# Selective scan: the column-order C values cross memory by 4-byte writes and whole-row reads instead of whole-row writes and 32-byte reads

## The chip, the cores and the metric

The kernel runs on one core of a Trainium2 chip. The metric is the device time of one launch in microseconds (us), lower is better. A launch computes the whole batch of 8 images, one image after the other.

## The reference

The input is `x` of 8 x 192 x 64 x 64 floats. Layer 0 is a state-space block: a layer norm over the channels, a projection to 384 channels (192 for the scan, 192 for a gate), a 3x3 depthwise convolution, and then a selective scan over the 4096 pixels in four directions. Layer 1 is a non-local attention block over the same pixels. What matters here is the scan:

```python
x_hw = xc.reshape(Bsz, D, L)                          # pixels row by row
x_wh = xc.transpose(0, 1, 3, 2).reshape(Bsz, D, L)    # pixels column by column
xs = jnp.stack([x_hw, x_wh, x_hw[..., ::-1], x_wh[..., ::-1]], axis=1)
x_dbl = jnp.einsum('kcd,bkdl->bkcl', x_proj_w, xs)
dts, Bv, Cv = jnp.split(x_dbl, [R, R + N], axis=2)    # 12, 4 and 4 rows per direction
...
dA = jnp.exp(dt_t[..., None] * A)
h = dA * h + dt_t[..., None] * B_t[:, :, None, :] * u_t[..., None]
y = jnp.einsum('bkdn,bkn->bkd', h, C_t)
```

For each direction k and each pixel there are four values C (one per state), the same for all 192 channels. Directions 0 and 2 go over the rows of the picture, directions 1 and 3 over its columns.

## The kernel before, in words

An image goes through three stages with a barrier behind each: project and scan, mix (output projection, and the projections of the attention), attend. The scan works in 32 chunks of 512 pixels: `ORDER = (0, 2, 1, 3)` gives the directions, 8 chunks each. A chunk's place in this list is called `at`. Places 0 to 15 (`at < EV`) are the row directions, where a chunk is 8 rows of the picture; places 16 to 31 are the column directions, where it is 8 columns.

`run_chunks` writes the code of each engine's `body` out 32 times; every engine has its own fixed order, and semaphores tie them. In `body(at)`:

- PE (TensorE) makes the projected rows of place at+2 (`xdbl`, only while at+2 < 16), the time-step rows (`dtproj`), spreads the C rows of this place over all 128 partitions (`spread`, line 478: a selection matrix times the tile `xhl[at % 2]`) and sums the products over the states.
- ACT (ScalarE) copies the small rows of place at+2 out of PSUM (`copy_xd`, line 786), computes the decay factors (`decay`, line 824), and copies the rows into `xhl` (`copy_high`, line 797). `xhl` holds in one tile the high part of the C rows and, 64 partitions further, the rest that DVE subtracts in `low_half` (line 1154). So there are two sets of rows, high and low.
- POOL (GpSimd) finishes the time step of place at+1 (`residue`, line 1011), multiplies it by the input (`times_u`, line 1017), and multiplies that by the spread B rows, in three `drive` operations (line 1026).
- DVE (VectorE) runs six scans (line 1175) and three products with C (line 1183) a chunk, and between them one step of the softplus for the next place (`softplus`, line 1165).
- SP issues every DMA. For each place it writes the four B rows to memory (line 329, tensor `rows`, with a wait for that write in line 330), and reads them back spread over 128 partitions (lines 332 and 335, tile `bs`).

The projection of a row chunk also yields the C values of directions 1 and 3 for the same pixels, 2 x 4 rows in both the high and the low set. They are kept in memory until the column directions need them. `STORE = (3, 5, 7, 9, 11, 13, 14, 15)` are the eight places at which SP stores a chunk of them to the tensor `ct` of 16 rows x 4096 pixels: two DMAs of 8 rows (line 339), issued once `low_half` of this place is done. At places 16 to 31 SP reads 4 + 4 of these rows for 8 columns of the picture back into `xhl` (line 350), once PE has finished reading the tile for place at-2 (the count of `cbc_ready`).

Three waits hang on the stores. SP itself goes on with the B rows of the next place only after it has issued the store. ACT may not overwrite `xhl` in `copy_high(at + 2)` until the store of place at has landed (`c_stored1`). At place 16 SP waits for all stores of the image before the first read. ACT's `copy_xd(at)` in turn waits until the B rows of place at-1 have been written out (`rows_saved`), and POOL's first `drive` of a place waits until its `bs` tile has been loaded (`b_loaded`).

Of the kernel before, what the change touches and what calls it, by code (L numbers as in the profile page):

```python
# [19 lines left out]
F32 = mybir.dt.float32  # L20
# [5 lines left out]
B, C, HH, WW = 8, 192, 64, 64  # L26
L = HH * WW
P = 128
R = C - P
NS, RANK, K = 4, 12, 4  # L30
O = 96
T = 512
NCH = L // T
RPC = T // WW
# [5 lines left out]
EV = 2 * NCH  # L40
STORE = (3, 5, 7, 9, 11, 13, 14, 15)
# [13 lines left out]
def build(nc, nb, x, vec, w_in, w_x, w_dt, sel, fold, ident, w_out, w_att, gb, w_w, out):  # L55
# [3 lines left out]
    with ctx:  # L59
# [29 lines left out]
        selr = sb("selr", [P, NT * P], F32R)  # L89
# [21 lines left out]
        def flat(ap):  # L111
            return ap.rearrange("p (a b) -> p a b", b=WW)
# [49 lines left out]
        xhl = [sb(f"xhl{i}", [P, T], F32R, where=scx) for i in range(2)]  # L162
# [6 lines left out]
        h = sb("h", [P, NT, T], where=scx)  # L169
# [3 lines left out]
        ps = ctx.enter_context(nc.psum_tensor("ps", [P, 8, T], F32))  # L173

        rden = nc.dram_tensor("rden", [T], F32, kind="Internal").ap()
        ct = nc.dram_tensor("ct", [4 * NS, L], F32, kind="Internal").ap()
# [39 lines left out]
        for w, rows_ in ((wx0, slice(0, P)), (wx1, slice(P, 2 * P))):  # L216
            for s, k in enumerate((0, 2)):
                at = s * P
# [73 lines left out]
        @block.sync  # L292
        def _(sp):
            sp.wait_ge(S["pads_set"], 11)
            for dst, src in LOADS:
                sp.dma_start(dst, src).then_inc(s_load, 16)
            sp.wait_ge(s_load, NL)
            barrier(sp, 0, -1)

            def load(im, i, c, q):  # L300

                sp.wait_ge(S["x_free"], i + 1)
                sl = bass.ds(c * T, T)
                sp.dma_start(xa[:, q, :], xr[im, 0:P, sl]).then_inc(S[f"x_loaded{q}"], 16)
                sp.dma_start(xb[0:R, q, :], xr[im, P:C, sl]).then_inc(S[f"x_loaded{q}"], 16)

            for q in range(2):
                load(0, q, q, q)
            with sp.Fori(0, nb) as b:
                sp.wait_ge(S["out_stored"], b * (32 * NCH) + 32)  # L310
                sp.sem_inc(mark, 1)
                with sp.Fori(1, NCH // 2) as cc:
                    for q in range(2):
                        load(b, (b * 2) * NCH + cc * 2 + q, cc * 2 + q, q)
                sp.wait_ge(S["xc_ready"], b * NCH + NCH)
                sp.sem_inc(mark, 1)

                def body(at, par, g, before, now, nxt, after):
                    k, c = now
                    if at < EV:  # L320
                        sp.wait_ge(S["xd_ready"], b * EV + (at + 1))
                        src = xd[RANK:RANK + NS, :]
                    else:
                        if at == EV:
                            sp.wait_ge(S["xs_ready"], b * NCH + NCH)
                        m = LO + 16 * (k // 2) + RANK
                        src = xsf[m:m + NS, bass.ds(c * T, T)]
                    sp.wait_ge(S["dbu_ready"], g * NP + 1)
                    sp.dma_start(rows[par], src).then_inc(S["rows_saved"], 16)
                    sp.wait_ge(S["rows_saved"], g * 16 + 32)  # L330
                    whole = rows[par].rearrange("n t -> (n t)").unsqueeze(0).to_broadcast([P, NS * T])
                    sp.dma_start(bs[par][:, 0:2, :, :].rearrange("p q e t -> p (q e t)"), whole).then_inc(S[f"b_loaded{par}"], 16)
                    for half in range(2):
                        part = rows[par].rearrange("(e w) t -> w e t", w=2)[half:half + 1].to_broadcast([R, 2, T])
                        sp.dma_start(bs[par][half * R:half * R + R, 2, :, :], part).then_inc(S[f"b_loaded{par}"], 16)
                    if at in STORE:
                        sp.wait_ge(S["xlo_ready"], b * EV + (at + 2))
                        for m, row in ((0, NX), (2 * NS, R + NX)):
                            sp.dma_start(ct[m:m + 2 * NS, c * T:(c + 1) * T], xhl[par][row:row + 2 * NS, :].bitcast(F32))\
                                .then_inc(S[f"c_stored{par}"], 16)  # L340
                    if at >= EV:
                        if at == EV:
                            sp.wait_ge(S["c_stored0"], b * 32 + 32)
                            sp.wait_ge(S["c_stored1"], b * (32 * 7) + 32 * 7)
                        sp.wait_ge(S["cbc_ready"], g * NP + 1)
                        for m, row in ((0, RANK + NS), (2 * NS, R + RANK + NS)):
                            m += NS * (k // 2)
                            src = ct[m:m + NS, :].rearrange("r (h w) -> r h w", w=WW)[:, :, c * RPC:(c + 1) * RPC]
                            dst = xhl[par][row:row + NS, :].bitcast(F32).rearrange("p (h w) -> p h w", w=RPC)
                            sp.dma_start(dst, src).then_inc(S[f"c_loaded{par}"], 16)  # L350
                run_chunks(sp, b, body)
                barrier(sp, b, 0)
                with sp.Fori(0, NCH // 2) as cc:
                    for q in range(2):
                        load(b, (b * 2 + 1) * NCH + cc * 2 + q, cc * 2 + q, q)
                barrier(sp, b, 1)
                for q in range(2):
                    load((b + 1) % nb, (b * 2 + 2) * NCH + q, q, q)

                def store(c):  # L360
                    sp.wait_ge(S["fin_ready"], (b * NCH + c) * 2 + 4)
                    sl = bass.ds(c * T, T)
                    sp.dma_start(outr[b, 0:P, sl], fa[:, 0, :]).then_inc(S["out_stored"], 16)
                    sp.dma_start(outr[b, P:C, sl], fa[0:R, 1, :]).then_inc(S["out_stored"], 16)

                def attend(c, par, before, nxt):

                    i = b * NCH + c
                    d = b * (NCH - 1) + c
                    if before:  # L370
                        sp.wait_ge(S["yraw_ready"], i + 1)
                        sp.dma_start(dcol[:, :], yraw[O:O + 1, :].rearrange("o (p j) -> o p j", j=4)).then_inc(S["den_loaded"], 16)
                        sp.wait_ge(S["rden_ready"], i)
                        sp.dma_start(rden.rearrange("(p j) -> p j", j=4), rcol[:, :]).then_inc(S["den_saved"], 16)
                        sp.wait_ge(S["den_saved"], d * 16)
                        sp.dma_start(rdb[:, :], rden.unsqueeze(0).to_broadcast([O, T])).then_inc(S["rb_loaded"], 16)
                        store(c - 1)
                    if nxt:
                        sp.wait_ge(S["nmx_ready"], i + 2)
                        for t in range(4):  # L380
                            sp.dma_start(thc[1 - par][0][O:O + 1, t * P:(t + 1) * P].bitcast(F32), nmr[:, t:t + 1].bitcast(F32))\
                                .then_inc(S["shift_loaded"], 16)
                run_attend(sp, attend)
                store(NCH - 1)
                barrier(sp, b, 2)
            sp.wait_ge(S["out_stored"], nb * (32 * NCH) + 32)
            for q in range(2):
                sp.wait_ge(S[f"x_loaded{q}"], nb * (32 * NCH) + 32)
# [3 lines left out]
        def _(pe):  # L392
            mm = pe.matmul
# [9 lines left out]
            with pe.Fori(0, nb) as b:  # L403
# [64 lines left out]
                def spread(q, k, c, at, g):  # L468

                    pe.wait_ge(S["hc_ready"], g * NP + (q + 3))  # L470
                    if q == 0 and at < EV:
                        pe.wait_ge(S["xlo_ready"], b * EV + (at + 2))
                    if q == 0 and at >= EV:
                        pe.wait_ge(S[f"c_loaded{at % 2}"], b * (32 * NCH) + 32 * ((at - EV) // 2 + 1))
                    for e in range(2):
                        j = 2 * q + e
                        src = flat(xhl[at % 2][:, :]) if at < EV else xhl[at % 2][:, :].rearrange("p (h w) -> p w h", w=RPC)
                        m = mm(flat(ps[:, 4 + e, :]), selr[:, j * P:(j + 1) * P], src, start=True, stop=True)  # L478
                    m.then_inc(S["cbc_ready"], 1)

                def sum_first(k, c, g):
# [236 lines left out]
        def _(act):  # L718
# [10 lines left out]
            with act.Fori(0, nb) as b:  # L729
# [62 lines left out]
                def copy_high(at, g):  # L792

                    act.wait_ge(S["cbc_ready"], g * NP + 1)
                    if at - 2 in STORE:
                        act.wait_ge(S["c_stored1"], b * (32 * 7) + 32 * (STORE.index(at - 2) + 1))
                    A(xhl[at % 2][:, :], ps[:, 0, :], ACT.Copy).then_inc(S["xhi_ready"], 1)

                def soft_abs(g):
# [642 lines left out]
```

## Time and profile before

| | us |
|---|---|
| median of 3 runs | 9575.38 (9568.02 to 9575.95) |
| the profiled execution, device time | 9585.77 |
| the profiled execution, span of the trace | 9583.9 |
| TensorE busy | 8813.6 (92%) |
| VectorE busy | 7318.6 (76%) |
| ScalarE busy | 6190.6 (65%) |
| GpSimd busy | 3294.3 (34%) |

The span runs from the first to the last instruction; the device time has 1.9 us more around it. The shares are averages over stages of different kinds: in the attention TensorE is busy all the time and GpSimd does nothing, in the scan VectorE and GpSimd carry much more than their average. The first image takes about one eighth of the span, its scan lies between 175 and 640 us from the start, and the other seven repeat it.

### The profile page before, as it was taken

The numbers are of one execution on the slowest core, as the hardware profiler recorded it, in microseconds if no ns is written. First come the engines' busy times: TensorE is split into PE (matmuls) and PEld (weight loads), VectorE is DVE, ScalarE is ACT, GpSimd is POOL, SyncE is SP. The second block draws the span as 40 slices with busy tenths as digits, with TensorE's granted clock in tenths as the row PEclk, the third lists the DMA queues.
The fourth block names the chain that finished last, engine by engine and source line by source line (L and its number), as shares of the span: only waits on it lengthen the run. The fifth ranks groups of instructions, "written<-read, shape, count | busy, mean of one in ns | idle before, by whom it ended". The sixth has DMA issues, their size and how long they took to land. (4 is left out here: it accounts for less than half of the span.)

```text
span 9583.9 us, 104556 instructions
## 1 busy us (share of the span) xinstructions
PE 8813.6 (92%) x26564; PEld 4729.1 (49%) x26564; DVE 7318.6 (76%) x8161; ACT 6190.6 (65%) x7500; POOL 3294.3 (34%) x1874
## 2 busy tenths in 40 slices
PE   7899988999889998899988999889998899989999
PEld 3336733367333673336733367333673336633366
DVE  6977769777697767977679776797767977679776
ACT  6765667656676566755667656675566755677555
POOL 2860028500385003850038500385003850048400
PEclk9999999999999999999999999999999999999999
DMA  1320013200132002320013200132002320023200
GB/s 52 114 77 12 11 54 112 72 12 11 54 114 72 11 10 61 109 71 11 12 59 113 68 10 12 59 114 67 10 12 63 110 67 10 12 66 114 60 11 12
DMA packets 286701, 503.35 MB, mean 53 GB/s; under 512 B 142155, under 2 KB 143215, under 8 KB 253431
## 3 DMA queue, kind: packets, MB, share of 16 engines
q1 hardware_dynamic: 286199, 497.81, 17.4%
q8 instruction: 174, 2.85, 0.1%
q14 instruction: 328, 2.69, 0.1%
HBM read 467.99 MB, written 29.47 MB: 52 GB/s over the span
## 5 line engine op out<-in xcount | busy, mean ns | idle before, releaser
L1313 DVE TENSOR_TENSOR pl<-pf,ph 128x1024 fp32r<-128x1024 f32 x1024 | 1254.6, 1225 | 1014.1 <-ACT ph L961 1006.3
L1175 DVE TENSOR_TENSOR_SCAN h<-ps,h,dbu 128x512 f32<-128x512 f32 x1536 | 1886.8, 1268 | 65.9 <-POOL dbu L1026 29.9
L1026 POOL TENSOR_TENSOR dbu<-bs,du 128x1024 f32<-128x1024 f32 x768 | 1800.9, 2375 | 54.1 <-POOL du L1017 54.1
L961 ACT ACTIVATE ph<-pf 128x1024 fp32r<-128x1024 f32 x1024 | 1086.5, 1061 | 753.0 <-PE ps L652 752.7
L955 ACT ACTIVATE pf<-ps 128x1024 f32<-128x1024 f32 x1024 | 1051.5, 1027 | 534.9 <-PE ps L639 534.9
L981 POOL MEMSET sqb<- 64x512 f32 x16 | 8.3, 520 | 3998.1 <-issue 3993.2
L824 ACT ACTIVATE ps<-dt,negA 128x512 f32<-128x512 f32 x1536 | 1038.3, 688 | 494.5 <-DVE h L1175 494.1
L1297 DVE TENSOR_REDUCE mx<-ps 128x1 f32<-128x512 f32 x1792 | 1168.9, 684 | 78.4 <-PE ps L557 60.4
L1183 DVE TENSOR_TENSOR hc<-h,ps 128x1024 f32<-128x1024 f32 x768 | 938.0, 1221 | 194.9 <-PE ps L478 113.5
L478 PE MATMUL ps<-xhl,selr 128*128 128x512 f32 x1536 | 847.8, 639 | 147.7 <-DVE hc L1183 147.5
L1011 POOL TENSOR_TENSOR dt<-dt,ze 128x1024 f32<-128x1024 f32 x256 | 605.9, 2367 | 923.7 <-ACT dt L817 923.5
L1017 POOL TENSOR_TENSOR du<-dt,u 128x512 f32<-128x512 f32 x512 | 714.3, 1417 | 567.2 <-DVE dt L1165 566.6
L637 PE MATMUL ps<-thc,phh 97*128 97x512 f32 x2048 | 845.7, 413 | 6.7 <-ACT thc L938 6.7
L650 PE MATMUL ps<-ph,gth 128*97 128x512 f32 x2048 | 817.4, 399 | 11.7 <-DVE pl L1313 8.6
L638 PE MATMUL ps<-thc,phl 97*128 97x512 f32 x2048 | 815.3, 398 | 0.0
L639 PE MATMUL ps<-thc,phh 97*128 97x512 f32 x2048 | 812.9, 397 | 0.0
L652 PE MATMUL ps<-pl,gth 128*97 128x512 f32 x2048 | 808.6, 395 | 0.0
L651 PE MATMUL ps<-ph,gtl 128*97 128x512 f32 x2048 | 807.5, 394 | 0.0
L557 PE MATMUL ps<-phh,thc 96*128 96x512 f32 x1824 | 633.6, 408 | 45.2 <-POOLq L187 18.8
L478 PEld LDWEIGHTS ps<-xhl,selr 128*128 128x128 f32 x1536 | 271.3, 196 | 631.0 <-DVE hc L1183 370.5
L505 PE MATMUL ps<-hc,foldw 128*128 128x512 f32 x1024 | 548.1, 662 | 0.0
L489 PE MATMUL ps<-hc,eye 128*128 128x512 f32 x1024 | 484.3, 595 | 0.0
(191 smaller groups left out, 14691.2 us busy)
## 6 DMA issues: line engine op xcount, KB each, us to landing
bs<-rows SPq DMA_DIRECT2D x256, 1024.0 KB, 5.2
bs<-rows SPq DMA_DIRECT2D x512, 256.0 KB, 6.1
xa<-in_x SPq DMA_DIRECT2D x130, 256.0 KB, 2.9
xb<-in_x SPq DMA_DIRECT2D x130, 128.0 KB, 3.0
out<-fa SPq DMA_DIRECT2D x64, 256.0 KB, 2.1
rdb<-rden SPq DMA_DIRECT2D x56, 192.0 KB, 3.4
out<-fa SPq DMA_DIRECT2D x64, 128.0 KB, 2.4
xhl<-ct SPq DMA_DIRECT2D x256, 8.0 KB
```

Of the source, the lines that this page charges most:

```text
L478: m = mm(flat(ps[:, 4 + e, :]), selr[:, j * P:(j + 1) * P], src, start=True, stop=True)
L637: mm(dst, kk, thc[par][0][:, :], start=True, stop=False)
L638: mm(dst, phl[:, m * P:(m + 1) * P], thc[par][0][:, :], start=False, stop=False)
L650: mm(dst, gth[:, m, :], ph[:, mp % 2, e, :], start=(m == 0), stop=False)
L824: A(ps[:, 2 + e, :], dt[par][:, 0 if j < NS else 1, :], ACT.Exp, scale=negA[:, k * NT + j:k * NT + j + 1]).then_inc(S["dA_ready"], 1)
L955: A(pf[:, mp % 2, :, :], ps[:, 2 * (mp % 2):2 * (mp % 2) + 2, :], ACT.Exp)\
L961: A(ph[:, mp % 2, :, :], pf[:, mp % 2, :, :], ACT.Copy).then_inc(S["ph_ready"], 1)
L1026: pool.tensor_tensor(dbu[:, q, :, :], bs[par][:, q, :, :], du[:, r:r + 1, :].to_broadcast([P, 2, T]), ALU.mult).then_inc(S["dbu_ready"], 1)
L1175: dve.tensor_tensor_scan(h[:, j, ::step], ps[:, 2 + e, ::step], dbu[:, q, e, ::step], h[:, j, end:end + 1], ALU.mult, ALU.add)\
L1183: TT(hc[:, q, :, :], h[:, 2 * q:2 * q + 2, :], ps[:, 4:6, :], ALU.mult).then_inc(S["hc_ready"], 1)
L1297: dve.tensor_reduce(mx[:, t, m:m + 1], ps[:, 5 + j % 2, :], AX.X, ALU.max)\
L1313: TT(pl[:, mp % 2, :, :], pf[:, mp % 2, :, :], ph[:, mp % 2, :, :].bitcast(F32), ALU.subtract)\
```

## The change

A store no longer writes rows of 512 pixels in picture order. It writes each value to its place in column order, so that `ct` holds the 4096 pixels of each row column by column. Neighbours of a source row are 64 values apart in memory, so every piece written is one value of 4 bytes. Each of the 16 rows of a store has a DMA of its own (16 DMAs of 512 pieces in place of 2 DMAs of 8 rows). The read at places 16 to 31 becomes a plain read of 4 rows of 512 values. The chunk then lies in `xhl` in column order, and the `spread` matmul reads it straight, where it used to step through it with a stride of 8 values. The counts of the semaphores `c_stored0` and `c_stored1` follow the number of DMAs.

```diff
@@ SP, body
                     if at in STORE:
                         sp.wait_ge(S["xlo_ready"], b * EV + (at + 2))
                         for m, row in ((0, NX), (2 * NS, R + NX)):
-                            sp.dma_start(ct[m:m + 2 * NS, c * T:(c + 1) * T], xhl[par][row:row + 2 * NS, :].bitcast(F32))\
-                                .then_inc(S[f"c_stored{par}"], 16)
+                            for n in range(2 * NS):
+                                dst = ct[m + n:m + n + 1, :].rearrange("r (w h) -> r h w", h=HH)[0, c * RPC:(c + 1) * RPC, :]
+                                src = xhl[par][row + n:row + n + 1, :].bitcast(F32).rearrange("p (h w) -> p h w", w=WW)
+                                sp.dma_start(dst.unsqueeze(0), src, allow_slow_non_contiguous=True).then_inc(S[f"c_stored{par}"], 16)
                     if at >= EV:
                         if at == EV:
-                            sp.wait_ge(S["c_stored0"], b * 32 + 32)
-                            sp.wait_ge(S["c_stored1"], b * (32 * 7) + 32 * 7)
+                            sp.wait_ge(S["c_stored0"], b * 256 + 256)
+                            sp.wait_ge(S["c_stored1"], b * (256 * 7) + 256 * 7)
                         sp.wait_ge(S["cbc_ready"], g * NP + 1)
                         for m, row in ((0, RANK + NS), (2 * NS, R + RANK + NS)):
                             m += NS * (k // 2)
-                            src = ct[m:m + NS, :].rearrange("r (h w) -> r h w", w=WW)[:, :, c * RPC:(c + 1) * RPC]
-                            dst = xhl[par][row:row + NS, :].bitcast(F32).rearrange("p (h w) -> p h w", w=RPC)
-                            sp.dma_start(dst, src).then_inc(S[f"c_loaded{par}"], 16)
+                            src = ct[m:m + NS, c * T:(c + 1) * T]
+                            sp.dma_start(xhl[par][row:row + NS, :].bitcast(F32), src).then_inc(S[f"c_loaded{par}"], 16)
@@ PE, spread
                     for e in range(2):
                         j = 2 * q + e
-                        src = flat(xhl[at % 2][:, :]) if at < EV else xhl[at % 2][:, :].rearrange("p (h w) -> p w h", w=RPC)
-                        m = mm(flat(ps[:, 4 + e, :]), selr[:, j * P:(j + 1) * P], src, start=True, stop=True)
+                        m = mm(ps[:, 4 + e, :], selr[:, j * P:(j + 1) * P], xhl[at % 2][:, :], start=True, stop=True)
@@ ACT, copy_high
                     if at - 2 in STORE:
-                        act.wait_ge(S["c_stored1"], b * (32 * 7) + 32 * (STORE.index(at - 2) + 1))
+                        act.wait_ge(S["c_stored1"], b * (256 * 7) + 256 * (STORE.index(at - 2) + 1))
```

On SP's queue, at place 13 and up to the B rows of place 15, this stood before (`ct<-xhl` is the store, `rows<-xd` and `bs<-rows` the B rows of the place that follows; in brackets the semaphore that a DMA waits for):

```order
L339 DMA ct<-xhl1 8x512 [waits xlo_ready]
L339 DMA ct<-xhl1 8x512
L328 ISA [waits xd_ready]
L329 DMA rows0<-xd 4x512 [waits dbu_ready]
L330 ISA
L332 DMA bs0<-rows0 128x2048 [waits rows_saved]
L335 DMA bs0<-rows0 64x2x512 x2
L337 REGISTER_ALU
L339 DMA ct<-xhl0 8x512 [waits xlo_ready]
L339 DMA ct<-xhl0 8x512
L328 ISA [waits xd_ready]
L329 DMA rows1<-xd 4x512 [waits dbu_ready]
```

And this stands there now:

```order
L342 DMA ct<-xhl1 8x64x1 [waits xlo_ready]
L342 DMA ct<-xhl1 8x64x1 x15
L328 ISA [waits xd_ready]
L329 DMA rows0<-xd 4x512 [waits dbu_ready]
L330 ISA
L332 DMA bs0<-rows0 128x2048 [waits rows_saved]
L335 DMA bs0<-rows0 64x2x512 x2
L337 REGISTER_ALU
L342 DMA ct<-xhl0 8x64x1 [waits xlo_ready]
L342 DMA ct<-xhl0 8x64x1 x15
L328 ISA [waits xd_ready]
L329 DMA rows1<-xd 4x512 [waits dbu_ready]
```

The B rows of places 14 and 15 stand behind 16 DMAs each where they stood behind 2; nothing changed its place. At place 16, the first of a column direction, SP's queue before had the reads of C in 64 pieces of 8 values a row:

```order
L335 DMA bs0<-rows0 64x2x512 x2
L343 REGISTER_ALU
L344 ISA [waits c_stored0]
L350 DMA xhl0<-ct 4x64x8 [waits cbc_ready,c_stored1]
L350 DMA xhl0<-ct 4x64x8
```

and now it has whole rows:

```order
L335 DMA bs0<-rows0 64x2x512 x2
L345 REGISTER_ALU
L346 ISA [waits c_stored0]
L351 DMA xhl0<-ct 4x512 [waits cbc_ready,c_stored1]
L351 DMA xhl0<-ct 4x512
```

The reads stand where they stood, with the same waits. The order on PE, ACT, POOL and DVE is the same as before.

## Rows read from the trace of the kernel before

**Rows 1.** The page: span, and busy time of each engine.

```profile
span 9583.9 us, 104556 instructions
PE 8813.6 (92%) x26564; PEld 4729.1 (49%) x26564; DVE 7318.6 (76%) x8161; ACT 6190.6 (65%) x7500; POOL 3294.3 (34%) x1874
```

**Rows 2.** Busy time of each engine in stretches (row and column places, first image).

```profile
core 0: us, PE busy (x) PEld busy (x) DVE busy (x) ACT busy (x) POOL busy (x), PEclk, DMA share, GB/s
219.00:391.00 172.00, 152.11 (x357) 63.10 (x356) 165.20 (x144) 133.67 (x185) 140.08 (x73) 1.00 0.34 112
420.00:636.00 216.00, 201.69 (x388) 74.57 (x386) 196.74 (x168) 159.08 (x194) 185.50 (x91) 0.97 0.34 104
```

**Rows 3.** SP in order of time, first image, places 7 and 13 to 15.

```profile
start us, us, engine line op out<-in xcount [idle before <-releaser]
275.38 0.61 SPq L339 DMA_DIRECT2D ct<-xhl  x2
279.41 0.24 SPq L329 DMA_DIRECT2D rows<-xd  x1
280.79 0.34 SPq L332 DMA_DIRECT2D bs<-rows  x1
281.18 1.24 SPq L335 DMA_DIRECT2D bs<-rows  x2
...
304.27 0.61 SPq L339 DMA_DIRECT2D ct<-xhl  x2
...
362.33 0.61 SPq L339 DMA_DIRECT2D ct<-xhl  x2
...
376.82 0.61 SPq L339 DMA_DIRECT2D ct<-xhl  x2
...
391.32 0.61 SPq L339 DMA_DIRECT2D ct<-xhl  x2
```

**Rows 4.** DMA issues of the page: size, median us from issue to landing.

```profile
bs<-rows SPq DMA_DIRECT2D x512, 256.0 KB, 6.1
```

**Rows 5.** POOL in order of time: places 8 and 14 to 16.

```profile
291.54 2.34 POOL L1011 TENSOR_TENSOR dt<-dt,ze 128x1024 f32<-128x1024 f32 x1
296.26 2.50 POOL L1017 TENSOR_TENSOR du<-dt,u 128x512 f32<-128x512 f32 x2 [2.39 <-DVE dt L1165]
299.01 7.03 POOL L1026 TENSOR_TENSOR dbu<-bs,du 128x1024 f32<-128x1024 f32 x3 [0.25 <-POOL du L1017]
...
400.49 7.03 POOL L1026 TENSOR_TENSOR dbu<-bs,du 128x1024 f32<-128x1024 f32 x3 [0.17 <-POOL du L1017]
...
416.47 7.02 POOL L1026 TENSOR_TENSOR dbu<-bs,du 128x1024 f32<-128x1024 f32 x3 [0.25 <-POOL du L1017]
```

**Rows 6.** DVE, then ACT, in order of time, beside these.

```profile
294.87 1.22 DVE L1165 SCALAR_TENSOR_TENSOR dt<-ps,dt 128x1024 f32<-128x1024 f32 x1
...
293.10 0.57 ACT L786 ACTIVATE xd<-ps 20x512 f32<-20x512 f32 x1
```

**Rows 7.** Issue time on SP in ns (least, median, most) of three lines.

```profile
L339 SPq DMA_DIRECT2D ct<-xhl x128: 268/290/298, 217.3 to 8738.8; - x128
...
L350 SPq DMA_DIRECT2D xhl<-ct x256: 622/640/731, 405.0 to 8968.8; - x128
...
L381 SPq DMA_DIRECT2D thc<-nmr x224: 516/596/1554, 821.3 to 9515.2; - x112
```

**Rows 8.** DMA between 420 and 423.5 us (two reads of C).

```profile
DMA packets 520, 0.02 MB, mean 5 GB/s; under 512 B 520, under 2 KB 520, under 8 KB 520
q1 hardware_dynamic: 520, 0.02, 8.3%
```

**Rows 9.** DMA between 217.5 and 219.5 us (two stores of C).

```profile
q1 hardware_dynamic: 32, 0.03, 9.1%
```

**Rows 10.** Who waited for whom: DVE, 420 to 636 us.

```profile
DVE hc L1183 <- PE ps L478: 13.2, 14, 1.5
```

**Rows 11.** The spread matmul in a row place and in a column place.

```profile
285.76 1.03 PE L478 MATMUL ps<-xhl,selr 128*128 128x512 f32 x2
...
417.96 1.03 PE L478 MATMUL ps<-xhl,selr 128*128 128x512 f32 x2
```

## The prediction

> **What bounds the kernel now.** I read the page first: TensorE is busy 92% of the span, the others less [rows 1]. That average belongs mostly to the attention, which the change does not touch, so the next view is the busy time by stretch. In the row places of the scan VectorE is busy 165.20 of 172.00 us and GpSimd 140.08 [rows 2]: DVE sets the pace, one place in about 14.5 us (the stores at 275.38 and 304.27 are two places apart [rows 3]). In the column places DVE is busy 196.74 of 216.00 us. Who waited for whom says why: 13.2 us of that is DVE waiting for the spread matmul, in 14 waits [rows 10].
>
> Then the queue that the change fills, SP in order of time. At place 7 the store takes 0.61 us, from 275.38; SP then waits, issues the B rows of place 8 at 279.41 and their spread reads until 282.42 (281.18 + 1.24) [rows 3]. The last read lands 6.1 us after its issue [rows 4], that is at 281.80 + 6.1 = 287.9, 8.5 us after the B rows were issued. The first user is POOL's `drive` of place 8, which begins at 299.01 [rows 5]. So the queue has some 11 us of slack, and what matters is how much of it the store eats.
>
> How much may POOL be late? It has an idle gap of 2.39 us a place, but in front of `times_u`, where it waits for DVE's line 1165. From `drive` it runs without a gap into the next `residue`; one such is 291.54 to 293.88, and DVE's line 1165, which needs it, starts at 294.87 [rows 5, 6]. So the slack is 1.0 us: a `drive` over 1.0 us late stops DVE, and DVE has nothing to give back.
>
> **The change, part by part.** Call S the time that SP needs to issue one store, now 0.61 us, then 16 DMAs of 512 pieces each.
>
> *An isolated store (places 3, 5, 7, 9, 11).* The B rows of the next place are issued at 275.4 + S, landed 8.5 us later, and needed at 299.0 + 1.0 = 300.0. Free up to S = 16.1; beyond that each us of S is a us of DVE. There are five, since the slip also moves the next store and the time until it, 28.9 us, lets the queue recover. ACT's `copy_xd` of place 9 starts at 293.10 and needs the B rows of place 8 saved, 1.4 us after their issue: that begins to slip at S = 16.3, the same point, and is no separate cost [rows 3, 6].
>
> *The three stores at the end (13, 14, 15).* They stand one place apart, 362.33, 376.82, 391.32 [rows 3]. Between two stores SP needs 3.0 us for the B rows (282.42 - 279.41), so from S = 11.5 the second and third start late. The B rows of place 15 land at 362.3 + S + 3.0 + S + 8.5 = 373.8 + 2S against 400.5 + 1.0; those of place 16 at 362.3 + 3S + 6.0 + 8.5 = 376.8 + 3S against 416.5 + 1.0 [rows 5]. The second rules: a loss of 3S - 40.7 from S = 13.6 on, which takes in what place 13 loses. It is paid once an image, since behind it SP has no stores and recovers.
>
> So an image loses 5 x (S - 16.1) + (3S - 40.7) us, and there are eight.
>
> *S itself.* No row shows DMAs of 512 single values. A DMA of 8 pieces takes 290 ns to issue, one of 256 pieces 640 ns [rows 7]: 1.41 ns a piece, and 1.00 us for 512, S = 16.0. Line 381 writes 128 single values in 596 ns [rows 7]: 2.55 ns a piece beyond the 8, and 1.58 us for 512, S = 25.2. If the pieces cost the queue nothing, S = 16 x 0.29 = 4.6, the lower end. I take 1.2 us a DMA, between the two and nearer to the row with 256 pieces, the nearest to 512 in count: S = 19.2.
>
> *The transfers.* Two reads of C make 520 packets: 512 pieces and 4 completions a DMA of 4 rows [rows 8]. Two stores make 32: 16 rows and 8 completions a DMA of 8 rows [rows 9]. So a DMA runs on as many of the 16 DMA engines as its outer dimension has entries, and the new one (8 x 64 x 1) on 8: 64 pieces each, 1024 an engine and store. A 32-byte piece cost 8.3% x 16 x 3.5 us / 520 = 8.9 ns [rows 8], so 1024 take 9.2 us, less than S, in its shade. The other end is the only row on writes of these rows, 9.1% x 16 x 2 us / 16 = 182 ns for 2 KB [rows 9]: S = 186 and some 11 ms more. A piece of 4 bytes is far nearer to the first in what it carries, and I take 8.9 ns.
>
> [...]
>
> *The reads.* 256 DMAs of 256 pieces become DMAs of 4: about 0.35 us of SP and 1.2 us of four DMA engines each. They are issued a whole place before their tile is read, and no engine is shown waiting for them. I count 0; bounds 0 and, if all of it lay in the open, 128 x 0.7 = 90 us gained, which nothing shows.
>
> *The matmul.* Two spread matmuls take 1.03 us with a straight read (285.76) and 1.03 us with the stride of 8 values (417.96) [rows 11]. So the stride costs nothing, 0.
>
> **The sum.** 5 x (19.2 - 16.1) = 15.5, 3 x 19.2 - 40.7 = 16.9, together 32.4 us an image, 259 us a launch. Against the profiled execution, 9585.8 + 259 = 9845; this lies 10.4 above the median of the runs, so 9835.
>
> **The rivals.**
>
> *The store stays hidden.* If a DMA issues in up to 0.85 us, S is below 13.6 and nothing is lost: 9575. For it: 0.24 to 0.34 us is what the DMAs of lines 329 and 332 take [rows 3], and those of line 332 have at least 128 pieces. Against: line 350 takes 640 ns for half the pieces.
>
> *The pieces, not the queue, set S.* Writes of 4 bytes to scattered addresses may cost a DMA engine far more than a read of 32, and with 1024 on each engine every nanosecond is a microsecond a store. The engines' queues fill and SP waits, or the B rows wait behind the pieces. It decides from about 19 ns a piece. At 30 ns S is 31: 5 x 14.9 + 52.3 = 127 us an image, 10,590; at 40 ns 207 us, 11,230. For it: 2 KB written took 182 ns. Against: 8.9 ns where a small piece is shown.
>
> *The matmul gets faster.* DVE waits 13.2 us an image for the spread matmul in the column places [rows 10]; if a straight read shortened that to nothing and the stores were hidden, 8 x 13.2 = 106 us would go, 9470. Against: 1.03 and 1.03. [...]
>
> **Chances and numbers.** Forecast (the queue, S from 16 to 25): 0.55; hidden: 0.15; pieces: 0.23; faster matmul: 0.05; something else 0.02. The forecast's own range is 8 x 7.3 above the median, 9634, to 8 x 80.4 above it, 10,219. The likeliest rivals lie on both sides, so the range goes from 9570, which takes in the hidden case, to 10,400 (S = 28), and leaves out the slower part of the pieces. About 0.2% is what a measurement can tell from no change. Slower by more: the forecast, the pieces, and little else, 0.8; within: the hidden case, 0.14; faster: 0.06.
>
> **What would show it.** The store's DMAs take 1.0 to 1.6 us each on SP at intervals of the same size; the B rows of the even row places are issued about S behind the store; POOL's `drive` at places 4, 6, 8, 10, 12 begins some 4 us late and waits for a DMA; DVE waits for POOL's line 1011 or 1026; the largest gap stands at places 15 and 16. The column places run as before, and so does the attention. I am wrong if the store takes under 14 us, if a DMA issue takes far over 1.6 us with the DMA engines busy all the while, or if the column places get shorter.

## The result, and the profile after

| | before | after |
|---|---|---|
| median of 4 runs, us | 9573.59 | 10716.31 |
| ratio (95% interval) | | 1.119 (1.117 to 1.121) |
| span of the profiled execution, us | 9583.9 | 10718.6 |

The kernel became 1143 us slower, 143 us an image. I had forecast slower, at 9835 us, and the time lies above my range.

The page after, first the span and busy times, as in [rows 1], then the DMA packets:

```profile
span 10718.6 us, 105452 instructions
PE 8841.1 (82%) x26564; PEld 4789.4 (45%) x26564; DVE 7335.8 (68%) x8161; ACT 6171.1 (58%) x7500; POOL 3287.1 (31%) x1874
...
DMA packets 752629, 503.44 MB, mean 47 GB/s; under 512 B 608075, under 2 KB 609135, under 8 KB 719351
```

Each engine's busy time is within 0.4% of what it was, so the 1135 us by which the span grew are idle time. For TensorE the equality hides two changes that cancel: the spread matmul took 145 us less over the launch (703.0 against 847.8), and the rest took more. The busy times of the first image's row places from about the first store on, before and then after (columns as in [rows 2]):

```profile
219.00:420.00 201.00, 176.59 (x406) 74.17 (x406) 191.60 (x166) 152.79 (x211) 162.92 (x84) 0.97 0.34 112
```

```profile
219.00:556.00 337.00, 191.65 (x406) 79.16 (x406) 194.10 (x167) 154.74 (x213) 158.04 (x81) 0.80 0.28 61
```

The 406 matmuls took 15 us longer, at a granted clock of 0.80 in the mean against 0.97. In the mean over 220 to 232 us, with TensorE at work, the clock was 1.00; from 247 to 252 us, at the end of its pause behind the store, it was 0.50. TensorE waits for others in this stretch, so little of this need have reached the launch; how much did is not shown.

The next view is SP in order of time after, at places 3 to 5 of the first image (columns as in [rows 3]):

```profile
216.31 31.76 SPq L342 DMA_DIRECT2D ct<-xhl  x16
248.21 0.57 SPq L329 DMA_DIRECT2D rows<-xd  x1
252.14 0.35 SPq L332 DMA_DIRECT2D bs<-rows  x1
252.53 1.29 SPq L335 DMA_DIRECT2D bs<-rows  x2
254.04 0.31 SPq L329 DMA_DIRECT2D rows<-xd  x1
259.82 0.34 SPq L332 DMA_DIRECT2D bs<-rows  x1
```

A store holds SP for 31.76 us, where it took 0.61 [rows 3]; the eight stores of the image take 27.9 to 33.2 us, 30.6 in the mean. The B rows then need 3.9 us from issue to the next step (248.21 to 252.14), where they needed 1.4; behind the eight stores of the image it is 3.6 to 4.9. Read with windows that end ever later, the same store shows when its 16 DMAs leave SP:

```profile
216.31 0.75 SPq L342 DMA_DIRECT2D ct<-xhl  x1
216.31 1.45 SPq L342 DMA_DIRECT2D ct<-xhl  x2
216.31 3.34 SPq L342 DMA_DIRECT2D ct<-xhl  x3
```

The first two take 0.75 and 0.70 us, the third 1.89 and the other 13 on average 2.2. So an issue of 512 pieces takes 0.7 us as long as nothing holds it, and from the third on SP is held back. That it is the flow of the pieces that holds it is what the experiments below test.

Who pays for it stands in ACT's and in DVE's order of time:

```profile
252.14 0.59 ACT L786 ACTIVATE xd<-ps 20x512 f32<-20x512 f32 x1 [18.07 <-DMA rows<-xd]
```

```profile
253.34 1.28 DVE L1175 TENSOR_TENSOR_SCAN h<-ps,h,dbu 128x512 f32<-128x512 f32 x1 [15.15 <-ACT ps L824]
```

`copy_xd` of place 5 waits 18.07 us until the B rows of place 4 are out; a decay stands behind it on ACT, and DVE's scan waits 15.15 us for that. At other stores the wait comes over POOL, which waits for its B tile. Who waited for whom, over the launch, DVE and then POOL:

```profile
DVE h L1175 <- ACT ps L824: 688.0, 173, 16.0
DVE h L1175 <- POOL dbu L1026: 350.5, 28, 22.0
```

```profile
POOL dbu L1026 <- DMA bs<-rows: 1030.1, 53, 25.5
```

### The profile page after: what moved, and what is told of

Read it like the earlier page. It is cut to its first block and busy times, and to the rows that moved or that the text cites. A ratio compares the mean times of both kernels' runs of the same rounds, so it can differ in the third digit from the quotient of the medians.

```text
span 10718.6 us, 105452 instructions
## 1 busy us (share of the span) xinstructions
PE 8841.1 (82%) x26564; PEld 4789.4 (45%) x26564; DVE 7335.8 (68%) x8161; ACT 6171.1 (58%) x7500; POOL 3287.1 (31%) x1874
## 2 busy tenths in 40 slices
DMA packets 752629, 503.44 MB, mean 47 GB/s; under 512 B 608075, under 2 KB 609135, under 8 KB 719351
## 5 line engine op out<-in xcount | busy, mean ns | idle before, releaser
L1175 DVE TENSOR_TENSOR_SCAN h<-ps,h,dbu 128x512 f32<-128x512 f32 x1536 | 1898.9, 1270 | 1044.3 <-ACT ps L824 688.0
L478 PE MATMUL ps<-xhl,selr 128*128 128x512 f32 x1536 | 703.0, 540 | 411.6 <-DVE hc L1183 268.5
L466 PE MATMUL ps<-xd,wdt 128*128 128x512 f32 x512 | 365.0, 852 | 769.3 <-ACT xd L786 664.1
```

Source lines behind the costliest of these rows:

```text
L478: m = mm(ps[:, 4 + e, :], selr[:, j * P:(j + 1) * P], xhl[at % 2][:, :], start=True, stop=True)
L1175: dve.tensor_tensor_scan(h[:, j, ::step], ps[:, 2 + e, ::step], dbu[:, q, e, ::step], h[:, j, end:end + 1], ALU.mult, ALU.add)\
```

## The experiments

S is, as in the prediction, the time for which one store holds SP; it is given as the mean of the eight stores of the first image.

| run | a store's DMAs | pieces | S, us | ns a piece | launch, us |
|---|---|---|---|---|---|
| changed kernel | 16 of 8x64x1, one tile row each | 8192 of 4 B | 30.6 | 3.7 | 10,716 |
| e1 | 16 of 4x64x1, one row each | 4096 of 4 B | 15.2 | 3.7 | 9,700 |
| e2 | 16 of 8x32x1, one row each | 4096 of 4 B | 14.1 | 3.4 | 9,757 |
| e3 | 16 of 16x32x1, one row each | 8192 of 4 B | 25.8 | 3.1 | 10,427 |
| e5 | 16 of 480x1 to SBUF, one row each | 7680 of 4 B | 22.8 | 3.0 | 10,547 |
| e6 | 16 of 8x64x8, 8 rows each | 8192 of 32 B | 15.6 | 1.9 | 9,727 |
| e9 | 16 of 8x64x1, 8 tile rows each | 8192 of 4 B | 14.3 | 1.7 | 9,656 |

e1, e2, e5, e6 and e7 are one timed run each. e7, the kernels without reordered stores (e4, e8) and those that hide the store (e10, e11) follow in their place. No view names the engines that a DMA ran on. Their number is read, as in the prediction, from the packets that a DMA has beyond its pieces: 8 in the changed kernel (752,629 packets in all), e2 (490,517), e6 (752,917), e7 (745,517) and e9 (752,629), 4 in e1 (486,421), 16 in e3 (760,821) and e5 (728,085). Where engines are counted below, it is by this reading.

The expectations name three theories of what holds SP for 3.7 ns a piece. A: each DMA engine needs some 30 ns for a 4-byte write to memory. B: the side that makes or feeds the pieces needs 3.7 ns for each, whatever the engines. C: memory takes one 4-byte write in that time, whatever the engines.

**e1 and e2: half the pieces, on 4 engines and on 8.**

```diff
-dst = ...[0, c * RPC:(c + 1) * RPC, :]       # 8 picture rows x 64
+dst = ...[0, c * RPC:c * RPC + 4, :]         # e1: 4 x 64
+dst = ...[0, c * RPC:(c + 1) * RPC, 0:32]    # e2: 8 x 32
```

> Half of each store: 4 picture rows x 64 values, so 16 DMAs of 4x64x1, 256 pieces of 4 bytes each, still 64 pieces for each DMA engine that takes part, if a DMA runs on as many engines as its outer dimension has entries. The other half of C is left out (ct holds input values there). Theory A (the DMA engines drain 4-byte writes to memory at about 30 ns each, and SP is held back by full queues): pieces per engine are unchanged, so a store still takes SP about 30 us and the launch about 10,700 us. Theory B (the issuing side makes pieces at 3.7 ns each, whatever the engines): half the pieces, a store of about 15 us, the launch about 9,750 us.

> Half of each store the other way: 16 DMAs of 8x32x1, 256 pieces of 4 bytes each, 32 for each of 8 DMA engines. The other half of C is left out (ct holds input values there). Theories A (engines drain at 30 ns a piece) and B (issue at 3.7 ns a piece) both say about 15 us a store and 9,750 us; beside the run with 4x64x1, which has as many pieces, it is the control: A says that the two differ by some 950 us, B that they are the same.

Measured: 9,700 and 9,757 us, S 15.2 and 14.1. Theory A is out: with 64 pieces an engine, as many as in the changed kernel, the store takes half the time. Between these three kernels what counts is the number of pieces in all. e2 is the slower one although its S is shorter. SP's waits show where: over the launch it waits 464 us for its B rows to be written in e2 and 348 us in e1. What the store has left in the queues would explain it; that is not shown.

**e3: the same pieces on 16 engines.**

```diff
-dst = ct[m + n:m + n + 1, :].rearrange("r (w h) -> r h w", h=HH)[0, c * RPC:(c + 1) * RPC, :]
+i = c * 4 * NS + m + n
+dst = ct.rearrange("r l -> (r l)")[(i % 2) * 32768:(i % 2) * 32768 + 32768]\
+    .rearrange("(a b s) -> a b s", a=16, s=64)[:, 0:32, i // 2]
```

> The same 16 DMAs of 512 pieces of 4 bytes, 256 bytes apart in memory, but in one even series of 512, so that the outer dimension is a multiple of 16; the values land in another order than column order, so the C values of the column directions are permuted. Theory A: 32 pieces for each of 16 engines, a store of about 15 us, 9,750 us. Theory B: nothing changes, 30 us a store and about 10,720 us. A third, C (the memory takes so many 4-byte writes a second, whatever the engines): also no change, 10,720 us; the run of half the pieces on 4 engines would then be fast.

Measured: 10,427 us, 1.089 of before (1.087 to 1.091), S 25.8. The trace has 8 more packets a DMA (760,821 against 752,629, over 1024 DMAs), read as 16 engines taking part in place of 8. The addresses differ too: the parts of one DMA lie 8 KB apart, where in the changed kernel they are neighbouring values. Twice the engines took 16% off, not half. A second count against A; B and C both expected no change, and the small gain is neither's.

**e5: to SBUF in place of memory.**

```diff
+scr = sb("scr", [4 * NS, 2 * 480], where=scx)
-dst = ct[...]
+dst = scr[m + n:m + n + 1, :].rearrange("p (l s) -> p l s", s=2)[:, :, 1 if at == 14 else 0]
```

> The 16 DMAs of a store write their single values to a scratch tile in SBUF in place of memory (480 of the 512 values, 8 bytes apart; ct holds input values, so C of the column directions is left out). Theory B (each piece costs about 3.6 ns before it reaches memory, where pieces are made or fed to the DMA engines): a store still takes SP 480/512 x 30 = 28 us, the launch some 10,500 us. Theory C (memory takes one 4-byte write in 3.6 ns): the pieces go at the rate of the first two DMAs of a store, 0.7 us each, a store of 11 us, the launch about 9,540 us.

Measured: 10,547 us, S 22.8 for 480 of 512 pieces. Writes to memory are not needed for a price of 3 ns a piece, which speaks against C. It is a weak witness, though, as the packets of the two stores do not look alike. The DMA queue between 218 and 240 us in this run, and between 218 and 246 us in the changed kernel (packets, MB, share of 16 engines):

```profile
q1 hardware_dynamic: 6576, 0.03, 65.6%
```

```profile
q1 hardware_dynamic: 6830, 0.03, 11.0%
```

In the changed kernel that is 0.110 x 16 x 28 / 6830 = 7.2 ns of an engine a piece, and the engines are idle the rest. In this run the share between 218 and 225 us is 11.5% for 1832 packets, or 0.115 x 16 x 7 / 1832 = 7.0 ns a piece. The 65.6% comes from the end of the store: between 235 and 236 us the share is 440.6% for 488 packets. That is over 100% of the 16 engines, so there the times of packets overlap, and the share is no busy time. What these late packets wait for is not shown, so the two stores may have different limits. A DMA of 480 values ran on 16 engines, so the fairer neighbour is e3: for 480 pieces of 512 its store would take 24.2 us, against 22.8 here.

**e6: pieces of 32 bytes.**

```diff
+for n in range(8):      # 8 copies of the rows
+    dst = ct[n * 4 * NS + m:n * 4 * NS + m + 2 * NS, 2 * c * T:2 * (c + 1) * T]\
+        .rearrange("r (l s) -> r l s", s=16)[:, :, 0:8]
+    src = xhl[par][row:row + 2 * NS, :].bitcast(F32).rearrange("p (l s) -> p l s", s=8)
```

> 16 DMAs of 8x64x8 a store: as many pieces (512) and as many engines (8) as in the changed kernel, but each piece writes 32 bytes to memory, 64 bytes apart (8 copies of the 16 rows; the values are not those of column order). Theory B: 3.6 ns a piece whatever its size, a store of 30 us, 10,700 us. Theory C: if what costs is a write of less than some size, a store of about 11 us and 9,540 us; if memory counts writes, no change from the changed kernel.

Measured: 9,727 us, S 15.6, 1.9 ns a piece, with as many pieces on as many engines. Neither theory had half the price. Its first two DMAs leave SP in 0.78 us together, the 14 others take 1.08 us each on the first store, so SP is held back here too. The run differs from the changed kernel in two things: the piece is larger, and a DMA reads 8 partitions where the changed one reads one.

**e7: two DMAs, dense addresses.**

```diff
-for n in range(2 * NS): ...
+dst = ct[m:m + 2 * NS, 2 * c * T:2 * (c + 1) * T].rearrange("r (l s) -> r l s", s=2)[:, :, 0]
+sp.dma_start(dst, xhl[par][row:row + 2 * NS, :].bitcast(F32), ...)
```

> A store as 2 DMAs of 8x512x1 (4096 pieces of 4 bytes each, 8 bytes apart in memory, so dense where the changed kernel has 256 bytes between them) in place of 16. C of the column directions is input data. If the price is per piece (B, or C without regard to addresses), 8192 pieces take some 30 us and the launch 10,700 us, though SP may leave the two DMAs sooner and the B rows wait behind them in the queue. If the 16 issues or the scattered addresses were the price, it falls to below 13 us a store and 9,540 us.

Measured: 13,810 us, the slowest of all. SP in order of time:

```profile
219.98 36.84 SPq L342 DMA_DIRECT2D ct<-xhl  x2
256.97 29.94 SPq L331 DMA_DIRECT2D rows<-xd  x1
302.00 0.35 SPq L334 DMA_DIRECT2D bs<-rows  x1
```

The B rows are out 82 us after the store began, about 10 ns a piece. So the 16 issues were not the price, and addresses close together are no cure. Two things changed at once here, the distance (8 bytes in place of 256) and the length of a DMA (4096 pieces in place of 512), and no run tells them apart. Each DMA here reads 8 partitions, so that alone does not make a store fast.

**e9: each DMA takes one picture row of 8 tile rows.** The same values go to the same places as in the changed kernel.

```diff
-for n in range(2 * NS):
-    dst = ct[m + n:m + n + 1, :].rearrange("r (w h) -> r h w", h=HH)[0, c * RPC:(c + 1) * RPC, :]
-    src = xhl[par][row + n:row + n + 1, :]...
+for r_ in range(RPC):
+    dst = ct[m:m + 2 * NS, :].rearrange("r (w h) -> r w h", h=HH)[:, :, c * RPC + r_]
+    src = xhl[par][row:row + 2 * NS, r_ * WW:(r_ + 1) * WW].bitcast(F32)
```

> The same values to the same places as the changed kernel, in 16 DMAs of 512 pieces of 4 bytes, but each DMA takes one picture row of 8 rows of the tile (8 partitions x 64 values) in place of 8 picture rows of one tile row. The run with 32-byte pieces, which went at 1.9 ns a piece against 3.7, differed in two things: the size of the piece, and that it read 8 partitions. If the one source partition is the price: a store of about 15 us, about 9,750 us. If it is the piece of 4 bytes: 26 to 30 us a store, 10,400 to 10,700 us.

Measured: 9,656 us, 1.0084 of before (1.0062 to 1.0105), S 14.3. With as many pieces, as large, over as many engines (the trace has exactly as many packets, 752,629), the loss falls from 1143 to 81 us. e3 writes series of the same form, 512 values 256 bytes apart, from one partition a DMA, over twice the engines, and needs 25.8 us. What e9 has and e3, the changed kernel and e1, e2 and e5 have not is a source spread over 8 partitions. Against the changed kernel the writes are spread too: its DMA writes 8 neighbouring values at a time, e9's goes to 8 rows of `ct`, 16 KB apart. e3 spreads them 8 KB apart and stays slow, which speaks for the source, but e3 also runs on 16 engines; a run with one source partition, 8 engines and spread writes is missing. How fast the first 8 DMAs of e9's first store leave SP:

```profile
217.92 6.26 SPq L342 DMA_DIRECT2D ct<-xhl  x8
```

That is 0.78 us a DMA, near the 0.75 and 0.70 us of the first two in the changed kernel; the second eight take 0.97 us each. So in e9 S is mostly the time of the issues, and SP is held back little. The DMA queue in e9, between 218 and 232 us:

```profile
q1 hardware_dynamic: 7359, 0.03, 23.2%
```

That is the same 7.1 ns of an engine a piece, at twice the rate of the changed kernel (7359 packets in 14 us against 6830 in 28).

**e4 and e8: the straight matmul.** e4 is the changed kernel with the stores of before, e8 the kernel before with only the straight read of line 478. Neither puts the C values of the column directions into the right order; the amount of work is the same.

```diff
-src = flat(xhl[at % 2][:, :]) if at < EV else xhl[at % 2][:, :].rearrange("p (h w) -> p w h", w=RPC)
-m = mm(flat(ps[:, 4 + e, :]), selr[:, j * P:(j + 1) * P], src, start=True, stop=True)
+m = mm(ps[:, 4 + e, :], selr[:, j * P:(j + 1) * P], xhl[at % 2][:, :], start=True, stop=True)
```

> The changed kernel with the stores of before (2 DMAs of 8 rows in picture order); whole-row reads and the straight matmul stay, so the C values of the column directions come in the wrong order. It prices the other two parts of the change. My step: reads 0 and matmul 0, so 9,574 us, the time before. The rival that the matmul gets faster: down to 9,470 us, and the 13.2 us an image that DVE waits for line 478 shrink.

> The kernel before with only the straight read of the spread matmul in the column places; stores in rows and reads in 32-byte pieces as before, so C comes in the wrong order there. The run with row stores took 9,542 us, 33 less than before. If the matmul is what gained (its mean in the column places fell from 650 to 444 ns), this run takes about 9,542 us too. If it was the whole-row read that gained, 9,575 us.

Measured: 9,542.3 us, 0.9966 of before (0.9954 to 0.9978), and 9,545.5 us, 0.9969 (0.9958 to 0.9980). The matmul gains some 30 us (33 and 29), the whole-row reads nothing that can be told. Line 478 on PE in the column places, before and in e8 (ns, least, median, most):

```profile
L478 PE MATMUL ps<-xhl,selr x90: 607/650/1412, 420.6 to 634.2; 128*128 128x512 f32 x90
```

```profile
L477 PE MATMUL ps<-xhl,selr x92: 387/444/1355, 423.3 to 635.4; 128*128 128x512 f32 x92
```

and DVE's wait for it between 420 and 636 us in e8, 3.7 us, against 13.2 in [rows 10]:

```profile
DVE hc L1182 <- PE ps L477: 3.7, 4, 1.1
```

**e10 and e11: hiding the store.** e10 is e9 with a store in two halves; e11 is e9 with C stored at other places.

```diff
+if at - 1 in STORE: put(at - 1, before[1], 1)    # e10: second 8 DMAs, a place later
+if at in STORE: ...; put(at, c, 0)               # e10: first 8
```

```diff
+CSTORE = (1, 3, 5, 7, 9, 11, 13, 15)             # e11, for the stores of C alone
-if at in STORE:
+if at in CSTORE:
```

> The same DMAs as in the run with one picture row each, in two halves: 8 behind the B rows of their place and 8 behind the B rows of the next place, so that SP's queue is held half as long each time. If a store takes 15 us in all: 8 + 3 us of SP a place of 14.5, everything hidden, and with the straight matmul about 9,542 us. If it takes 30: 15 + 3 + 2.5 us a place, 20.5 against 14.5 at 13 places, so about 6 x 13 = 78 us an image and 10,170 us: still the queue, less by the waits that the long stores cause.

> The run with one picture row and 8 tile rows a DMA lost some 14 us an image, and its trace puts them behind the three stores at places 13, 14 and 15 and at the read of place 16. Here C is stored at every odd place (1, 3, ... 15), which also meets each of the 8 chunks once, so no two stores stand one place apart; everything computed stays the same. If the queue theory holds with a store of 14 us: the B rows of place 16 land at about 391.3 + 14.2 + 11 = 416.5 against 417.5, all stores hidden, and the gain of the straight matmul is left: about 9,545 us, 0.3% faster than before. If the pieces also cost by crowding the DMA engines beside the B loads, it stays near 9,600 us.

Measured: e10 9,601 us, 1.0026 of before (1.0015 to 1.0037), e11 9,551 us, 0.9973 (0.9962 to 0.9983). e10 missed its 9,542: between 400 and 440 us DVE waits for the first column places' C, since the halves pile up at places 14 to 16 (16 DMAs from 372.26 us, 16 from 392.93, 8 from 413.00). In e11 the same wait in the same stretch is 0.9 us; the 5 us between them, eight times, are most of the 59 us that e10 missed by.

```profile
DVE hc L1187 <- PE ps L482: 6.0, 3, 4.2
```

e11 came out as expected, with stores of 14 us still in it. SP at places 15 and 16:

```profile
391.67 13.96 SPq L343 DMA_DIRECT2D ct<-xhl  x16
406.08 0.27 SPq L330 DMA_DIRECT2D rows<-xsf  x1
407.95 0.34 SPq L333 DMA_DIRECT2D bs<-rows  x1
408.34 1.27 SPq L336 DMA_DIRECT2D bs<-rows  x2
409.80 0.68 SPq L351 DMA_DIRECT2D xhl<-ct  x2
```

It computes all that the reference asks, and is faster than both kernels: 0.27% below before.

## Why the prediction was wrong

**The bounds and the queue: right for a long store.** The slack of the B rows and who depends on them hold. Put into the prediction's formula, S = 30.6 gives 5 x 14.5 + 51.1 = 124 us an image, 989 in all. The B rows now take at least 2.5 us longer to be written (3.9 against 1.4), which the formula left out: that adds 2.5 to each of five stores and 7.5 at the end, 20 us an image, and brings 1149. Less the 30 of the matmul, 1119, against 1143 measured. The first image bears out the two parts: from the store of place 3 to that of place 13 it took 83 us longer (228.3 against 145.1), where five stores at 17.0 make 85; from there to the first load of the next stage it took 58 (351.0 against 293.2), where the end makes 51.1 + 7.5 less the matmul's 4, so 55. For short stores the formula gives too little: 3 x 14.3 - 40.7 = 2.2 us an image or 18 in all for e9, where the launch lost 81 us besides the 30 that the matmul gave back. There POOL's `drive` of places 15 and 16 waits 5.30 and 6.24 us for its B rows. The last three stores of e9 take 44.6 us together, more than 3 x 14.3, and the B rows behind them need 2.0 to 2.4 us to be written; with both the formula gives some 50 us, and the rest of the 111 is not explained. ACT's path over `copy_xd`, which I called no separate cost, was the one most often seen (688.0 us of DVE's waits against 350.5 over POOL), at about the same point, as worked out.

**S itself: the step that failed.** I made S of issue time alone, 1.2 us for a DMA of 512 values, S = 19.2, and put the transfers in its shade, at nothing. The 1.2 came from rows in which one or two DMAs of at most 256 pieces are issued into an empty queue [rows 7]. Such a row cannot show what 16 in a row cost. Both halves were off. An issue that nothing holds takes 0.70 to 0.78 us (the first two of a store, and the first eight in e9), so issue time alone would be some 12 us, below the 13.6 from which a store costs anything. From the third DMA on SP is held back to 2.2 us a DMA, a wait that the sum did not have, and S came to 30.6. Of the term 5 x (S - 16.1) + (3S - 40.7) only S was mis-sized, 19.2 for 30.6. That I forecast the right direction owes something to luck: with the true price of an issue my sum would have said that the store stays hidden.

**The transfers: wrong as a price, and the rival wrong as a mechanism.** I reckoned 8.9 ns of an engine a piece in parallel over 8 engines, 9.2 us a store [rows 8]. The busy time is about right (7.2 ns a piece after), but the engines are mostly idle (busy 11.0% between 218 and 246 us), and the store takes three times that. The rival "the pieces, not the queue, set S" came near in time (10,590 at 30 ns a piece and engine, measured 10,716), and is right in that the pieces hold SP: half of them take half the time. Its mechanism, a dear write at each engine, fell with e1, e2 and e3. The packets beyond the pieces, from which the prediction read how many engines a DMA runs on, follow the outer dimension in these runs too: 8 a DMA in the changed kernel (8x64x1), 4 in e1 (4x64x1), 16 in e3 (16x32x1). The number hardly mattered for the time. Shown is: 3.7 ns a piece for the whole queue in the changed kernel, and 1.7 when each DMA takes one picture row of 8 partitions. What in the chip holds the changed kernel's store stays open: the single source partition is the likeliest, the 8 writes side by side in memory are not fully ruled out, and I have no run with 32-byte pieces from one partition, which would tell the two differences of e6 apart. In e7, with 4-byte writes close together in long DMAs, yet another price appears, about 10 ns a piece.

**The matmul: wrong by a misread row.** I compared 1.03 us at 285.76 and 1.03 us at 417.96 [rows 11] and called the second a column place. It is the last spread of place 15, a row place with a straight read; the column places begin with the spread at 420.58, and there the median is 650 ns against 444. The stride costs about 0.2 us a matmul, 96 times an image. Over the launch DVE's wait for the spread fell from 113.5 us to 41.8 in e8, and the time fell by some 30, 4 us an image. So the 0 of the prediction rested on a row that shows no stride; the trace shows 607 ns at the least with the stride of 32 bytes against 387 without. What in the chip makes the stride cost is not shown. The rival on the matmul was right that the straight read is faster and shortens DVE's wait; the size was a third of its bound, 30 for 106 us.

**The reads: right,** nothing (e4 and e8 differ by 3 us, within their intervals). The 1.2 us of four DMA engines given there is that of a pair of reads, not of one; it entered no sum.

## What to carry to other kernels

The issue time of one DMA into an empty queue is the price of an issue that nothing holds; here it was good for the first two of a train of 16 (0.75 and 0.70 us, the third 1.89, the others 2.2 on average). For a train ask how many pieces flow per us for the whole queue, from the packets of a window, and look for what stands behind the train on the same engine. If a reordering write can't be avoided, try DMAs that each read several source partitions and write to places apart from each other, and place the trains where the queue has slack between them: with the same 8192 pieces a store the launch lost 1143 us (changed kernel, S 30.6), 81 us (e9, S 14.3), or nothing (e11). When two rows are to show that an access pattern is free, check that each belongs to the branch it is taken for.

## What the hardware showed

- 8192 single values from one partition a DMA: 30.6 us a store on 8 DMA engines (changed kernel), 25.8 on 16 (e3, in another order of addresses); from 8 partitions a DMA, to 8 rows of memory, on 8 engines: 14.3 us (e9). The numbers of engines here and below are read from the packets beyond the pieces.
- Half the pieces, from one partition a DMA, on 4 engines (e1, 15.2 us) and on 8 (e2, 14.1 us) take nearly the same.
- 8192 single values 8 bytes apart in memory, in 2 DMAs of 4096: about 82 us (e7).
- While SP was held back in the changed kernel (218 to 246 us), the 16 DMA engines were busy 11.0% in the mean, so the 8 that are read as taking part about 22%.
- In the row places of the changed kernel (219 to 556 us), with TensorE idle behind each store, its granted clock was 0.80 in the mean against 0.97 before (219 to 420 us).
- A float32r matmul of 512 columns whose moving rows have a stride of 32 bytes: 607 ns at the least (before), against 387 straight (e8).
